# One head of an attention kernel on TensorE: scores in two pairs, an output block of 256 columns, transposes for the fold

## The reference, cut to what matters

```python
bias = (rel_h[:, :, :, :, None] + rel_w[:, :, :, None, :]).reshape(b * heads, n, n)   # n = 1024 tokens
attn = jax.nn.softmax(jnp.einsum('bnd,bmd->bnm', q * scale, k) + bias, axis=-1)
out = jnp.einsum('bnm,bmd->bnd', attn, v)                                              # b * heads = 48
```

## Time and profile before

| | us |
|---|---|
| median of 3 runs (1133.24 to 1135.39) | 1134.29 |
| the profiled execution's own time | 1133.58 |
| its span, first to last instruction | 1131.8 |
| TensorE busy (share of the span) | 1024.3 (91%) |
| VectorE busy | 700.6 (62%) |
| ScalarE busy | 642.2 (57%) |
| POOL busy | 170.2 (15%) |
| mean granted TensorE clock, of full speed | 0.92 |

### The profile page before, as it was taken

One profiled execution on the slowest core, in us unless ns is written; L12 is line 12 of the kernel. 1 busy time (PEld: TensorE's weight loads), 2 busy tenths in 40 slices (PEclk: granted clock), 3 DMA queues, 4 the chain that ended last, 5 costly groups with the idle time before them and its releaser, 6 DMA issues. The chain is left out here.

```text
span 1131.8 us, 23833 instructions
## 1 busy us (share of the span) xinstructions
PE 1024.3 (91%) x7112; PEld 622.0 (55%) x7112; DVE 700.6 (62%) x1074; ACT 642.2 (57%) x1308; POOL 170.2 (15%) x273
## 2 busy tenths in 40 slices
PE   4899969999999999999999999987665599999995
PEld 2566634444444444444444444436665477887884
DVE  6765477777777777777777777722533444444442
ACT  3564327777777777777777777774211344444441
POOL 4420000000000000000000000004210144444442
PEclk8997659999999999999999999998755699999998
DMA  5256965344344544443354445206960011111110
GB/s 151 56 139 252 235 140 74 74 91 89 75 73 90 87 75 73 91 87 75 73 90 88 75 73 90 55 2 204 242 154 23 21 51 53 52 46 50 55 44 2
DMA packets 74988, 101.07 MB, mean 89 GB/s; under 512 B 26927, under 2 KB 43806, under 8 KB 73414
## 3 DMA queue, kind: packets, MB, share of 16 engines
q1 hardware_dynamic: 64244, 80.13, 33.7%
q0 software_dynamic: 10256, 19.80, 6.2%
q10 hardware_dynamic: 450, 0.66, 0.3%
HBM read 72.28 MB, written 30.05 MB: 90 GB/s over the span
## 5 line engine op out<-in xcount | busy, mean ns | idle before, releaser
L774 DVE TENSOR_REDUCE neg_max<-max_ps 128x1 f16<-128x1024 f32 x384 | 452.4, 1221 | 81.6 <-PE max_ps L620 81.6
L754 ACT ACTIVATE probs<-ring_ps 128x512 f32<-128x512 f32 x768 | 407.7, 602 | 76.3 <-PE ring_ps L652 75.5
L652 PE MATMUL ring_ps<-q_side,k_side 113*128 113x512 f16 x768 | 262.0, 383 | 1.8 <-ACT probs L754 1.5
L620 PE MATMUL max_ps<-k_side,q_side 112*128 112x256 f16 x1536 | 237.0, 277 | 8.9 <-ACT ident L721 6.6
L661 PE MATMUL out_ps<-probs,values 128*32 128x512 f32 x1536 | 204.6, 604 | 9.8 <-issue 9.8
L620 PEld LDWEIGHTS max_ps<-k_side,q_side 112*128 112x128 f16 x1536 | 150.0, 98 | 95.5 <-DVE neg_max L774 8.1
L652 PEld LDWEIGHTS ring_ps<-q_side,k_side 113*128 113x128 f16 x768 | 63.9, 101 | 114.9 <-ACT probs L754 98.2
L1351 DVE TENSOR_TENSOR hidden<-hid_ps,silu 118x128 f32<-118x128 f32 (+1 forms) x156 | 45.2, 290 | 107.3 <-ACT silu L1317 95.5
L1317 ACT ACTIVATE silu<-hid_ps 118x128 f32<-118x128 f32 (+1 forms) x156 | 42.5, 273 | 108.6 <-PE hid_ps L1260 107.1
L1257 PE MATMUL hid_ps<-slot_t,w_top 128*118 128x128 f32 (+1 forms) x624 | 103.2, 289 | 0.6 <-ACT slot_t L1298 0.6
L604 POOL COPY values<-v_sb 128x136 f32 (+1 forms) x48 | 14.4, 304 | 558.4 <-PE out_ps L661 558.4
(11 more groups left out here) (178 smaller groups left out, 1014.8 us busy)
## 6 DMA issues: line engine op xcount, KB each, us to landing
q_side<-rel_split SPq DMA_DIRECT2D x384, 64.0 KB, 3.2
q_side<-qk_split SPq DMA_DIRECT2D x144, 128.0 KB, 3.5
rel_split<-rel_hi SPq DMA_DIRECT2D x6, 1024.0 KB, 4.7
rel_split<-rel_lo SPq DMA_DIRECT2D x6, 1024.0 KB, 7.2
k_side<-qk_split SPq DMA_DIRECT2D x144, 32.0 KB, 3.6
w_top_all<-in_w_t POOLq DMA_DIRECT2D x2, 1876.0 KB, 16.3
qk_split<-att_sb SPq DMA_DIRECT2D x24, 128.0 KB, 2.4
q_side<-max_rows SPq DMA_DIRECT2D x192, 2.0 KB
```

The source lines that it names most:

```text
L620: last = nc.tensor.matmul(max_ps[t % 2][:, keys], q_side[slot][0:MAX_ROW, quarter, t * P:(t + 1) * P], k_side[slot][0:MAX_ROW, keys], star ...
L652: nc.tensor.matmul(ring_ps[at % 3][:], k_side[s.slot][:, tile * P:(tile + 1) * P], q_side[s.slot][:, tile // 2, (i % 2) * HALF:(i % 2 + 1) ...
L754: nc.scalar.activation(probs[:, u % 2 * GROUP + i, :], ring_ps[score_at(GROUP * u + i) % 3][:], ACT.Exp).then_inc(exp_done, 1)
L774: nc.vector.tensor_reduce(neg_max[:, slot % 2, t:t + 1], max_ps[t % 2][:], AX, ALU.max, negate=True).then_inc(tile_max, 1)
```

## The change

- **Rows.** The 112 rows of `q_side` and `k_side` are laid out anew (key parts at rows 0, 48 and 64, one-hot rows behind the first and the last). Which part of q stands at 0 and which at 64 differs between the first two and the last two quarters. `fill` becomes `load_products` (8 DMAs, ahead of `store_max`) and `load_positions` (8 DMAs, behind it): 16 DMAs, the same bytes. `raw_scores` keeps its 4 matmuls of 256 columns over 112 rows.
- **Maxima.** POOL repeats a head's maxima four times (`repeat_max`), TensorE transposes 128x32 instead of 128x8, ScalarE copies 32 rows, SP stores them with one DMA instead of four. `transpose_max` waits for POOL, and so does the reuse of `neg_max` on VectorE.
- **Weighted values.** `out_ps` has 256 columns: each of its four strips holds a quarter of the queries, and both key tiles of a group are added into it. A group is 8 matmuls of 256 columns instead of 4 of 512. `copy_out` copies 256 columns, and now stands behind the fourth exponential of u = 0 instead of ahead of the third of u = 1.
- **Fold.** Nothing is left to add, so `turn_out` is 2 transposes of 128x128. `copy_fold` goes: VectorE reads the transposed block in the ring's bank, and the bank is free at `att_done`. `normalize` moves between the two maxima of u = 2.
- **Order.** TensorE's group is: score, score, raw tile, raw tile, weighted values of the group before (with the two transposes behind them), score, score. `copy_max` stands behind the sixth exponential. The turns of the maxima and of the transposes are 6 and 11 of 18 instead of 8 and 13.

```diff
-def fill(sp, g, n, head, slot):
+def load_products(sp, g, head, slot):
     q, k, inc = g.q_side[slot], g.k_side[slot], g.loaded[slot]
-    both = lambda ap: ap.rearrange("r (o n) -> r o n", o=1).broadcast_to([ap.shape[0], 4, N])
+    copies = lambda ap, times: ap.rearrange("r (o n) -> r o n", o=1).broadcast_to([HD, times, N])
     q_hi, q_lo, k_hi, k_lo = (g.qk_split[i, part, bass.ds(slot * D + head * HD, HD), :] for i in range(2) for part in range(2))
-    for at, src in ((0, q_hi), (HD, q_hi), (2 * HD, q_lo)):
-        sp.dma_start(q[at:at + HD, :, :], both(src)).then_inc(inc, 16)
-    for at, src in ((0, k_hi), (HD, k_lo), (2 * HD, k_hi)):
+    for at, src in ((0, k_hi), (K_LO, k_lo), (LOWER, k_hi)):
         sp.dma_start(k[at:at + HD, :], src).then_inc(inc, 16)
-    for part in range(2):
-        for axis in range(2):
-            at = 3 * HD + (2 * part + axis) * HS
-            halves = g.rel_split[axis, part, :, head, slot, :].rearrange("(a r) n -> r a n", a=2)
-            dst = q[at:at + HS, :, :].rearrange("p (i j) n -> p i j n", i=2)
-            for other in range(2):
-                where = dst[:, :, other, :] if axis == 0 else dst[:, other, :, :]
-                sp.dma_start(where, halves).then_inc(inc, 16)
+    sp.dma_start(q[K_LO:K_LO + HD, :, :], copies(q_hi, 4)).then_inc(inc, 16)
+    for i in range(2):
+        for at, src in ((0, (q_hi, q_lo)[i]), (LOWER, (q_lo, q_hi)[i])):
+            sp.dma_start(q[at:at + HD, 2 * i:2 * i + 2, :], copies(src, 2)).then_inc(inc, 16)
...
+def load_positions(sp, g, head, slot):
+    q, inc = g.q_side[slot], g.loaded[slot]
+    for i in range(2):
+        quarters = slice(2 * i, 2 * i + 2)
+        for part in range(2):
+            at = LOWER if part != i else 0
+            rows, cols = (g.rel_split[axis, part, :, head, slot, :].rearrange("(a r) n -> r a n", a=2) for axis in range(2))
+            sp.dma_start(q[at + HD:at + HD + HS, quarters, :], rows[:, i:i + 1, :].broadcast_to([HS, 2, N])).then_inc(inc, 16)
+            sp.dma_start(q[at + HD + HS:at + HD + 2 * HS, quarters, :], cols).then_inc(inc, 16)
+K_LO = HD + 2 * HS
+LOWER = 64
+MAX_ROW = LOWER + HD + 2 * HS
+ROWS = MAX_ROW + 1
+LOADS = 16
...
-        MAX_AT, FOLD_AT, TURN = 8, 13, 18
-        FOLDED = 4 * 4 * HD
-        folded_sb = sb("folded", [P, FOLDED])
-        def score_at(k):
-            return k + (k >= 8) + (k >= 12)
...
+    BANKS = 3
+    MAX_AT, TURNED_AT, TURN = 6, 11, 2 * KT + 2
...
+        out_ps = ctx.enter_context(nc.psum_tensor("out_ps", [P, QN], F32))
+        turned_ps, max_t_ps = ring_ps[TURNED_AT % BANKS][:, 0:2 * P], ring_ps[MAX_AT % BANKS][0:QUARTERS * KT, 0:P]
...
+        def turn_of(k):
+            at = k + (k >= MAX_AT)
+            return at + (at >= TURNED_AT)
...
-            def store_max(n, slot):
+            def store_max(n, j):
                 sp.wait_ge(max_copied, n + 1)
-                for quarter in range(QUARTERS):
-                    sp.dma_start(q_side[slot][MAX_ROW:ROWS, quarter, :].rearrange("o (t p) -> o t p", p=P),
-                                 max_rows[:, slot % 2, :]).then_inc(max_loaded[slot], 16)
+                sp.dma_start(q_side[j][MAX_ROW:ROWS, :, :].rearrange("o q (t p) -> o (q t) p", p=P), max_rows[:, j % 2, :]).then_inc(max_loaded[j], 16)
...
-                    fill(sp, g, s.n + 3, s.group + (s.slot + 3) // SLOTS, (s.slot + 3) % SLOTS)
+                    load_products(sp, g, head(s, 3), slot(s, 3))
                 if s.after(1):
-                    store_max(s.n + 1, (s.slot + 1) % SLOTS)
+                    store_max(s.n + 1, slot(s, 1))
+                if s.after(3):
+                    load_positions(sp, g, head(s, 3), slot(s, 3))
...
+            def repeat_max(n, j, reused):
+                pool.wait_ge(tile_max, KT * (n + 1))
+                if reused:
+                    pool.wait_ge(max_t_ready, n - 1)
+                pool.sem_inc(turn, 1)
+                copies = neg_max[:, j % 2, :].rearrange("p (o t) -> p o t", o=1).broadcast_to([P, QUARTERS, KT])
+                nc.gpsimd.tensor_copy(max_copies[:, j % 2, :, :], copies).then_inc(max_repeated, 1)
...
-                pe.wait_ge(tile_max, KT * (n + 1))
-                nc.tensor.matmul(ring_ps[MAX_AT % 3][0:KT, 0:P], neg_max[:, slot % 2, :], ident16[:],
+                    if at == TURNED_AT and s.before(1 + back):
+                        return pe.wait_ge(att_done, s.n - back)
+                    if at not in (MAX_AT, TURNED_AT):
+                        k = at - (at > MAX_AT) - (at > TURNED_AT)
+                        return pe.wait_ge(exp_done, 2 * KT * (s.n - back) + k + 1)
+                    at -= BANKS
+            def transpose_max(n, j):
+                pe.wait_ge(max_repeated, n + 1)
+                nc.tensor.matmul(max_t_ps, max_copies[:, j % 2, :, :].rearrange("p q t -> p (q t)"), ident16[:],
                                  start=True, stop=True).then_inc(max_t_ready, 1)
...
-            def weighted_values(n, slot, u):
-                pe.wait_ge(exp_done, 16 * n + GROUP * u + GROUP)
-                for i in range(GROUP):
-                    tile = 2 * u + i // 2
-                    last = nc.tensor.matmul(out_ps[i * 2 * HD:(i + 1) * 2 * HD, :], values[slot][:, tile, :],
-                                            probs[:, u % 2 * GROUP + i, :], start=(u == 0), stop=(u == PAIR_TILES - 1),
-                                            tile_position=(0, i * 2 * HD))
+            def weighted_values(n, j, u):
+                pe.wait_ge(exp_done, 2 * KT * n + GROUP * u + GROUP)
+                for i in range(2):
+                    tile = 2 * u + i
+                    for quarter in range(QUARTERS):
+                        queries = slice(quarter % 2 * QN, (quarter % 2 + 1) * QN)
+                        last = nc.tensor.matmul(out_ps[quarter * 2 * HD:(quarter + 1) * 2 * HD, :], values[j][:, tile, :],
+                                                probs[:, u % 2 * GROUP + 2 * i + quarter // 2, queries],
+                                                start=(tile == 0), stop=(tile == KT - 1), skip_group_check=True,
+                                                tile_position=(0, quarter * 2 * HD))
                 last.then_inc(group_done, 1)
-            def fold_out(n):
+            def turn_out(n):
                 pe.wait_ge(out_copied, n + 1)
-                for blk in range(4):
-                    last = nc.tensor.matmul(ring_ps[FOLD_AT % 3][:, blk * 4 * HD:(blk + 1) * 4 * HD], out_t[:, blk * P:(blk + 1) * P],
-                                            fold[:], start=True, stop=True, skip_group_check=True)
-                last.then_inc(folded, 1)
+                for b in range(2):
+                    last = nc.tensor.transpose(turned_ps[:, b * P:(b + 1) * P], out_t[:, b * P:(b + 1) * P], g.ident[:])
+                last.then_inc(turned, 1)
...
-                    for i in range(GROUP):
-                        scores(s, u, i)
-                        if i in (1, 2):
-                            if u == 0 and s.after(1):
-                                raw_scores(s.n + 1, one, 6 + i - 1, True)
-                            if u >= 1 and s.after(2):
-                                raw_scores(s.n + 2, two, 2 * (u - 1) + i - 1, True)
+                        pe.wait_ge(loaded[slot(s, 2)], 16 * LOADS * (head(s, 2) + 1))
+                    scores(s, u, 0)
+                    scores(s, u, 1)
+                    for i in range(2):
+                        if u == 0 and s.after(1):
+                            raw_scores(s.n + 1, slot(s, 1), 6 + i, True)
+                        if u >= 1 and s.after(2):
+                            raw_scores(s.n + 2, slot(s, 2), 2 * (u - 1) + i, True)
...
-                        bank_free(s, FOLD_AT)
-                        fold_out(s.n - 1)
+                        bank_free(s, TURNED_AT)
+                        turn_out(s.n - 1)
+                    scores(s, u, 2)
+                    scores(s, u, 3)
...
-            def copy_fold(n, reused):
-                act.wait_ge(folded, n + 1)
-                if reused:
-                    act.wait_ge(att_done, n)
-                nc.scalar.activation(folded_sb[:], ring_ps[FOLD_AT % 3][:, 0:FOLDED], ACT.Copy).then_inc(fold_copied, 1)
...
-                        if u == 1 and i == 2 and s.before(1):
+                        k = GROUP * u + i
+                        if i == 0 and (s.before(1) or u >= 2):
+                            act.wait_ge(group_done, PAIR_TILES * s.n + u - 1)
+                        act.wait_ge(scores_ready, 2 * KT * s.n + k + 1)
+                        nc.scalar.activation(probs[:, u % 2 * GROUP + i, :], ring_ps[turn_of(k) % BANKS][:], ACT.Exp).then_inc(exp_done, 1)
+                        if u == 0 and i == 3 and s.before(1):
                             copy_out(s.n - 1, s.before(2))
...
-            def normalize(n, head, image, reused):
-                dve.wait_ge(fold_copied, n + 1)
```

(43 more changed lines are left out.)

97 lines of the change are left out of this document (40 added, 57 removed).

## The result

| | before | after |
|---|---|---|
| median, us (lowest to highest, runs) | 1133.76 (1132.49 to 1135.39, 4) | 1191.12 (1187.91 to 1193.50, 4) |
| ratio, 95% interval | 1 | 1.0487 (1.0450 to 1.0524) |
| profiled execution and its span, us | 1133.58, 1131.8 | 1189.23, 1187.4 |
| mean granted TensorE clock | 0.92 | 0.92 |

The change makes the kernel 4.9% slower, some 57 us. I had forecast 1195.5 and a range of 1170 to 1238.

What follows compares the result with a forecast made beforehand. TensorE was taken to bound the attention stage, at 12.58 us a head. The terms sum to +1.32 us, a head of 13.90; 46 heads give +60.7, plus 1 once: 1195.5 us, range 1170 to 1238.

Steps and rivals of the forecast that it cites:

- copied output: Weighted values no longer wait for ScalarE's copy of the output block: -0.25 us a head.
- fold to transposes: On TensorE, eight fold instructions of 0.95 us become two transposes of 0.27 us: -0.68 us a head.
- weighted values: Four passes of 256 columns take 0.96 us against 0.90 a group: +0.21 us a head.
- three runs of four scores: Four scores on three banks: the fourth starts 1.08 us behind the first, stalling 0.42; +1.27 us a head.
- third score behind the transposes: It waits for VectorE to free the transposes' bank, starting at 1.19 instead of 0.71: +0.48 us a head.
- second raw tile behind VectorE: It waits for a VectorE reduction queued behind the division, till 2.35 instead of 2.06: +0.29 us a head.
- The two terms that I put at nothing: POOL's repeated max rows are hidden; position loads behind the max row's store arrive with 3 us in hand.
- Once per program: Two fills +1.9 us, POOL's first repeat +0.5, shorter end -1.3: about +1 us.
- (a): Rival, faster: the fourth score finds its bank free; -33 us, 1101 us; chance 0.05.
- (b): Rival, dear small matmuls: joins of weighted-value passes lie open, 0.88 us a head; +41, 1236 us; chance 0.12.
- (c): Rival, the clock falls as TensorE is less busy: +497 us if throughout, about 1690 us; chance 0.03.
- (d): Rival, late loads: TensorE waits in group 1, perhaps 1 to 2 us a head, 1240 to 1290 us; chance 0.03.

Runs made afterwards that it cites:

- experiment 3: Kernel before, with only ScalarE's output copy moved behind the fourth exponential of group 0: 1122.68 us, ratio 0.9887, a head of 12.35 us.
- experiment 1: Changed kernel, with the last two scores of a group ahead of the weighted values instead of behind them: 1095.49 us, ratio 0.9625, a head of 11.69 us.
- experiment 6: Changed kernel, with the eight position loads ahead of the store of the max row: 1192.21 us, measured once, a head of 13.75 us.
- experiment 4: Kernel before, with the new TensorE order and early output copy, keeping fold and 512-column matmuls: 1207.04 us, ratio 1.0627, a head of 14.11 us.
- experiment 2: Changed kernel, with TensorE's old order (score, score, raw tile, score, raw tile, score, weighted values): 1098.91 us, ratio 0.9677.

## Why the prediction was right

The direction and the size came from one term, and its mechanism is the one the runs show. Step by step, in us a head:

| step | forecast | measured |
|---|---|---|
| copied output | -0.25 | -0.23 (experiment 3) |
| fold to transposes | -0.68 | -0.67 (0.28 for the pair) |
| weighted values | +0.21 | 0.00 |
| three runs of four scores | +1.27 | +1.27 (1.08 each time) |
| third score behind the transposes | +0.48 | +0.47 (1.18 for 1.19) |
| second raw tile behind VectorE | +0.29 | +0.26 (1.30 for 1.04) |
| head | 13.90 | 13.75 |

The measured terms add up to 13.68, the head is 13.75. Most of the rest is in the same terms: over the whole stage the group with the transposes takes 3.88 us on average (3.74 to 3.96) where the head shown has 3.85, and each of the other three groups is 0.43 longer than in experiment 1 (3.28 against 2.85), not 0.42. The two terms that I put at nothing are nothing: the group with the max transpose takes 2.88 us with the repeated maxima (experiment 1) and without (experiment 3), and the landing of the loads holds nobody up (experiment 6).

**The term that was mis-sized** is the weighted values: "If that bit is fixed, a pass of half the columns costs 0.24: four make 0.96 against 0.90, +0.05 a group". A group to the next score takes 1.00 us after (401.58 to 402.58) as before (401.17 to 402.17). The small bit beyond the columns comes once a group, not once a pass: the four passes of the group at 401.58 start there and 0.24, 0.46 and 0.67 us later, so that a pass takes 0.24 once and 0.22 then. Even at 128 columns the group grows by 0.01 only. Four groups by 46 heads at 0.05 are 10 us too many. By the estimate from the figure of the Trainium skill (TensorE: Matmul & The Clock Gate, Measured speedup vs the span model), given beside that step, the head would have been 0.1 us shorter than my forecast. The trace agrees with that better than with the figure I preferred: the group stayed at 1.00 us. My lower bound, "nothing at all, if a pass costs by its columns alone", was the value.

**A reason that does not hold.** I put 0.06 of the 1.14 in the last head down to an exponential that waits for two things at once. The exponential behind the score at 402.17 waits for two as well and starts 0.43 us after it, as do all of its kind in the 40 heads of the loop that find ScalarE idle; only in the heads written out at the two ends is it 0.49. What makes that difference no run shows. The value that I took, 1.08, was the one for the loop.

**Once per program** I had about +1. Between the two traces it is about +3, but that is partly chance. At the start I had +2.4 and these two traces give +3.3. SP's own timeline shows the first fill of the projection, before and after:

```profile
111.32 2.07 SPq L507 DMA_DIRECT2D q_side<-qk_split  x3
```

```profile
112.27 3.24 SPq L509 DMA_DIRECT2D k_side<-qk_split  x3
```

The first three issues take 3.24 us instead of 2.07. The change did not make that: with the loads of before they take 3.28 and 3.29 in experiments 3 and 4, and with the new ones 2.18 in experiment 2. Over all profiled executions the first max transpose comes at 156.87 to 157.94 us with the old fills (three) and at 158.76 to 160.35 with the new (seven), +2.0 on average: 1.6 by the end of SP's last issue, where I had 1.9 for the four more DMAs, and 0.4 behind it, where I had 0.5 for POOL's repeat. So the step holds. At the end I forecast -1.3. From the last max transpose to the last product of the attention it is 21.54 before and 20.62 after, -0.9; what follows is the same code, and took 362.4 and 363.0 us here, and 362.3 to 370.5 in the ten profiled executions. An end-to-end time thus says little about a microsecond; the pitch of the heads does.

In sum: the attention stage got 52.7 us where I had 60.7, 8.0 too many; the weighted values alone are 9.7 of that, and what the terms fall short of the head gives 1.7 back. The two ends got 2.9 in these traces where I had 1.1. So the span came out 6.1 us under mine, 1187.4 for 1193.5. (The forecast's last addition is off by a little: 1134.29 and 61.7 make 1196.0, 1133.58 and 61.7 make 1195.3.)

**The rivals.** (a) falls: a bank came back after 1.08 us, not within 0.66, in the change and in experiment 4. But its arithmetic holds where no run of four is made: 1101 was its time, and the first two experiments, which have what it counts, took 1095.49 and 1098.91. (b) falls with a group of 1.00 us, at 256 and at 128 columns. (c) falls: the granted clock is 1.00 in the stretch with the stalls. The Trainium skill (TensorE: Matmul & The Clock Gate, A second HAM failure mode: psum-queue depth-cycling) describes a kernel whose clock swings because TensorE pauses while it cycles through banks. This case's traces do not agree: at four pauses of about 0.4 us in 13.7 the clock of the stretch from 300 to 400 us stayed at 1.00 in every run here. (d) falls: the loads land sooner than before (2.1 us, shown below, against 3.2), and experiment 6 moves them for nothing.

## What to carry to other kernels

Before reordering a queue, count the longest run of instructions that each fill a buffer of a ring, across the seam from one turn of the loop to the next, and set (time from a buffer's fill to its release) against (buffers times the pace of the run): here 1.08 against 0.66. Two runs of two, each harmless, made one run of four at the seam, and it cost more than all the instructions saved. The cure here was no new buffer (no run tried a fourth bank) but the same work in an order in which the long work that needs no bank stands between the runs.

## What the runs showed of the hardware

**Small matmuls side by side cost nothing here.** A group of weighted values streams the same columns as 4 matmuls of 512, 8 of 256 or 16 of 128 columns in 1.00, 1.00 and 1.01 us, though each matmul brings a weight load of some 0.11 us. At 128 columns the four loads of a pass start 7 ns apart while the pass ahead streams, and the passes follow one another at 0.109 us: the loads lie under it.

**The same bytes in less DMA time.** I had not expected the new layout to change the transfers. The page's queue line and its line of the position loads, before (the first) and after (the second and third):

```profile
q1 hardware_dynamic: 64244, 80.13, 33.7%
```

```profile
q1 hardware_dynamic: 65012, 80.13, 23.5%
...
q_side<-rel_split SPq DMA_DIRECT2D x384, 64.0 KB, 2.1
```

The columns are packets, MB and the share of 16 engines' span. For 80.13 MB in slightly more packets the engines are taken 279 us instead of 381 (share by span; 279 to 294 in all runs with the new loads, 375 to 387 in those with the old), and a 64 KB load lands in 2.1 us where it took 3.2. Experiment 4, which keeps the old layout in the new order, has the old landing of 3.2; experiment 6, without the store between the two sets of loads, has 2.1 still. So it is the form of the loads (rows, pieces, their order) and not the new order on TensorE or the store between them; which property of it stays open, and the single store of the maxima, which comes with the new form in every run, is not told apart from it. It is off the path and gained nothing here.
